# Mixture-of-experts rows placed by scatter in DRAM without index lists, and the decay mixer's constants moved among its first steps

## What is computed

```python
# L0_ffn: attention, then one of four experts for each row
x = x + _attn(x, ...)
h = _layernorm(x, ln2_w, ln2_b)
expert_idx = jnp.argmax(h @ router_w, axis=-1)
for e in range(4):
    gate_raw, value = jnp.split(h @ expert_wv[e], 2, axis=-1)      # 256 -> 2 x 1024
    y = gate_raw * sigmoid(gate_raw) * value @ expert_proj[e]       # 1024 -> 256
    out = out + jnp.where((expert_idx == e)[..., None], y, 0.0)
# L1_attn: the decay mixer: layer norm, W_in, a causal convolution of 4 taps, silu, a second norm,
# then a decaying mix whose rates come from A = clip(log(1 + exp(A_param)), 0.1, 10)
```

## Time and profile before

| What | us |
|---|---|
| three runs, lowest, median, highest | 3326.74, 3329.53, 3329.79 |
| the profiled execution's own time | 3336.9 |
| its span, from first to last instruction | 3335.1 |
| PE busy | 2797.5 (84%) |
| DVE busy | 2184.5 (65%) |
| ACT busy | 1569.1 (47%) |
| POOL busy | 1043.2 (31%) |

### The profile page before, as it was taken

How to read it: one execution, slowest core, us unless ns; L and a number is a source line. 1 busy time by engine, 2 the same in 40 slices (tenths; PEclk the granted TensorE clock), 3 DMA queues, 4 the chain that set the end, 5 groups by cost and what they waited for, 6 DMA issues and landing times.

```text
span 3335.1 us, 40739 instructions
## 1 busy us (share of the span) xinstructions
PE 2797.5 (84%) x13719; PEld 1686.9 (51%) x13782; DVE 2184.5 (65%) x3943; ACT 1569.1 (47%) x2311; POOL 1043.2 (31%) x705
## 2 busy tenths in 40 slices
PE   7778887787764699999966999948988887999999
PEld 3444454454452355555543666624444444666666
DVE  0698898899893676777532222226777775777776
ACT  2677667766761245555541111137777782111111
POOL 0887787788871111112102111012111100010000
PEclk9898998999866899999988999978999998999999
DMA  3354444454552744555323000010000002000000
GB/s 108 80 112 107 105 104 103 96 113 103 111 110 61 105 70 83 86 89 95 63 104 81 26 23 23 17 49 13 7 7 7 7 1 58 7 7 13 7 7 13
DMA packets 120347, 198.60 MB, mean 60 GB/s; under 512 B 15728, under 2 KB 78064, under 8 KB 118992
## 3 DMA queue, kind: packets, MB, share of 16 engines
q1 hardware_dynamic: 97504, 124.24, 16.5%
q0 software_dynamic: 22640, 71.75, 10.9%
HBM read 107.12 MB, written 25.91 MB: 40 GB/s over the span
## 4 chain that ended last, share of the span: by engine, by line
PE 51%; ACT 5%; DVE 5%; issue 4%; DMA 2%; POOL 0%; SPq 0%; ACTq 0%; DVEq 0%; POOLq 0%
PE PS L1517 7%; PE PS L2222 7%; PE PS L2240 6%; PE PS L1539 4%; PE PS L1810 3%; PE PS L1182 2%; PE PS L1859 2%; ACT Z L1963 2%; PE PS L1817 2%; PE PS L1161 2%; PE PS L1164 2%; PE PS L1109 1%; PE PS L1139 1%; PE PS L1877 1%; PE PS L1208 1%
## 5 line engine op out<-in xcount | busy, mean ns | idle before, releaser
L702 POOL TENSOR_TENSOR Z<-Z 128x1024 f32<-128x1024 f32 x256 | 652.7, 2661 | 109.5 <-PE PS L472 109.3
L652 DVE TENSOR_TENSOR_SCAN Z<-PS,Z 128x1024 f32<-128x1024 f32 x256 | 583.3, 2279 | 7.7 <-ACT PS L584 7.7
L472 PE MATMUL PS<-Z 128*128 128x128 f32 x2048 | 313.9, 301 | 139.8 <-DVE Z L665 131.9
L472 PEld LDWEIGHTS PS<-Z 128*128 128x128 f32 x2048 | 259.1, 156 | 288.4 <-DVE Z L652 145.2
L584 ACT ACTIVATE PS<-Z 128x511 f32<-128x511 f32 x512 | 332.2, 683 | 91.9 <-DVE Z L652 91.0
L1275 ACT ACTIVATE Z<-PS 128x512 f32<-128x512 f32 x320 | 189.1, 597 | 262.5 <-PE PS L1164 259.0
L2222 PE MATMUL PS<-Z 128*128 128x512 f32 x576 | 273.8, 600 | 17.5 <-DVE Z L2355 17.5
L440 PE MATMUL PS<-Z 128*128 128x512 f32 x512 | 254.6, 614 | 36.3 <-ACT Z L519 35.6
L2273 ACT ACTIVATE Z<-PS 128x512 f32<-128x512 f32 x144 | 86.0, 597 | 416.8 <-PE PS L2222 416.8
L1370 DVE TENSOR_REDUCE Z<-PS 128x1 f32<-128x512 f32 (+2 forms) x384 | 182.7, 508 | 114.6 <-PE PS L1140 109.9
L1963 ACT ACTIVATE Z<-Z 128x2048 f32<-128x2048 f32 x128 | 252.7, 2000 | 10.3 <-PE PS L1859 8.5
(11 more groups left out here) (278 smaller groups left out, 5021.6 us busy)
## 6 DMA issues: line engine op xcount, KB each, us to landing
Z<-Z POOLq DMA_DIRECT2D x120, 512.0 KB, 4.6
Z<-rows_b SPq DMA_DIRECT2D x128, 256.0 KB, 3.1
Z<-scr SPq DMA_DIRECT2D x256, 128.0 KB, 5.7
scr<-Z SPq DMA_DIRECT2D x32, 384.0 KB
Z<-in_L_ffn_expert_wv SPq DMA_DIRECT2D x4, 2048.0 KB, 14.6
rows_y<-Z SPq DMA_DIRECT2D x35, 128.0 KB, 1.7
Z<-in_L_attn_x SPq DMA_DIRECT2D x8, 512.0 KB, 8.9
rows_n<-Z SPq DMA_DIRECT2D x8, 512.0 KB, 2.9
```

Source lines behind the costliest of these rows:

```text
L472: ins = e.transpose(o[:, c * 128:(c + 1) * 128], self.h(k, c // 2)[:, c % 2, i * 128:(i + 1) * 128], ident)
L652: e.tensor_tensor_scan(h, a, h, 0.0, ALU.mult, ALU.add).then_inc(s["scan"], 1)
L702: e.tensor_tensor(self.h(k, f), self.du[b % 2][:, 2 * f:2 * f + 2, :], b3(self.Bs[k % 2], 1, [128, 2, 512]), ALU.mult).then_inc(s["hin"], 1)
```

## The change

The array `lists` and all that serves it go away: the cleared buffer, SP's write of it, the scatter of row numbers, the 35 gathers of row numbers. `rows_n` grows from 4096 rows to four regions of 4224 rows, one for each expert, and POOL scatters the normalized rows themselves (1 KB each) to their places; SP's eight stores to `rows_n` go. So that places which no row takes hold numbers, POOL first copies part of the expert weights over the whole array, in four transfers from DRAM to DRAM of 4.3 MB each, right after step `low` of group 4 in stage B. `nt` and `h2` change tiles, and the waits with them. SP loads `we` once two heads are turned. In stage D the constants' work becomes steps among the first block's steps, whose plan is one unit longer.

```diff
-        self.lists = m.nc.dram_tensor("lists", [NE * self.REG, 1], I32, kind="Internal").ap()
-        self.rows_n = m.nc.dram_tensor("rows_n", [4096, 256], F32, kind="Internal").ap()
+        self.rows_n = m.nc.dram_tensor("rows_n", [NE * self.REG, 256], F32, kind="Internal").ap()
...
-        e.wait_ge(s["zero"], 1)
-        e.dma_start(self.lists.rearrange("(p n) o -> p (n o)", p=128), self.zero).then_inc(s["d_l"], 16)
...
             elif p == 3:
                 e.wait_ge(s["nb"], b + 1)
                 if b < NB - 1:
-                    e.wait_ge(self.b.s["pj"], 2 * (b + 1))
+                    e.wait_ge(self.b.s["hc"], min(b + 4, NB) + 1)
+                if 0 < b < NB - 1:
+                    e.wait_ge(s["d_rows"], 64 * b)
...
+    def pool(self, e):
+        size = self.REG * 256
+        some = self.m.d["L0_ffn_expert_wv"].rearrange("x k m -> (x k m)")[0:size].rearrange("(p n) -> p n", p=128)
+        for x in range(self.NE):
+            e.dma_start(self.rows_n[x * self.REG:(x + 1) * self.REG].rearrange("(p n) c -> p (n c)", p=128),
+                        some).then_inc(self.s["d_fill"], 16)
...
             if p == 10:
                 e.wait_ge(s["posi"], b + 1)
-                if b == 0:
-                    e.wait_ge(s["ready"], 1)
-                    e.wait_ge(s["d_l"], 16)
+                e.wait_ge(s["d_fill"], 16 * self.NE)
             c = 4 * b + p - 10
-            e.indirect_dma_start(self.lists, bass.IndirectOffsetOnAxis(ap=self.posi[:, c:c + 1], axis=0),
-                                 self.ids[:, c:c + 1], None).then_inc(m.d_lists, 16)
+            e.indirect_dma_start(self.rows_n, bass.IndirectOffsetOnAxis(ap=self.posi[:, c:c + 1], axis=0),
+                                 self.nt[b][p - 10], None).then_inc(s["d_rows"], 16)
...
         def flipped(b):
             if b >= 4:
-                e.wait_ge(*self.made["route", b - 4, 6])
+                e.wait_ge(*self.made["route", b - 4, 4, 1])
+                e.wait_ge(self.route.s["d_rows"], 64 * (b - 3))
...
+            if g == 4:
+                self.route.pool(e)
...
-        e.wait_ge(self.route.s["posi"], NB)
+        e.wait_ge(s["ht"], 2)
         for x in range(self.NE):
             e.dma_start(self.we[:, 2048 * x:2048 * (x + 1)].rearrange("p (k m) -> p k m", k=8), ...
...
-        e.wait_ge(m.d_lists, 16 * 4 * NB)
-        e.wait_ge(self.route.s["d_rows"], 16 * NB)
+        e.wait_ge(self.route.s["d_rows"], 64 * NB)
         def rows(c):
-            e.wait_ge(*self.d_li.done(c))
             if c >= 4:
                 e.wait_ge(s["ht"], c - 3)
             e.indirect_dma_start(self.gr[c % 4], None, self.rows_n,
-                                 bass.IndirectOffsetOnAxis(ap=self.li[c % 4].bitcast(I32), axis=0)).then_inc(
+                                 bass.IndirectOffsetOnAxis(ap=self.start[:, c:c + 1], axis=0)).then_inc(*self.d_gr.over(c))
...
+    START = (
+        (("stats",), ("consts",)), (("rstd",), ("minus",), ("spread",)), (("norm",), ("decay",)), (("flip", 0), ("flip", 1)),
+        (("flipped", 0), ("flipped", 1), ("lift", 2)), (("lifted", 2), ("lift", 3)),
+        (("lifted", 3), ("taps", 2), ("lift", 0)), (("lifted", 0), ("taps", 3), ("lift", 1)), (("bound",),),
+        (("lifted", 1), ("conv", 0)), (("conved", 0), ("conv", 1))) + PLAN[10:]
```

More of the change, by code:

```diff
@@ L734, in __init__ @@
         self.upf = ar.take([128])
-        self.tab = ar.take([32 + 35 + 8 + 1 + 32])
-        self.ids = ar.take([32]).bitcast(I32)
+        self.tab = ar.take([32 + 35 + 8 + 1])
         self.oh = ar.take([32, 4])
@@ L988, in __init__ @@
         for b in range(NB - 1):
-            self.route.nt[b] = self.yf.rearrange("p a (b c) -> p (a b) c", c=256)
-            self.route.h2[b] = self.hp[:, :, 2:514]
+            self.route.nt[b] = [self.hp[:, i // 2, 2 + 256 * (i % 2):258 + 256 * (i % 2)] for i in range(4)]
+            self.route.h2[b] = self.yf
         self.end_use = {}
@@ L1081, in load @@
                                     self.d_stack[which][w % 3], 16)
-        self.walk(low=low, load=load, route=self.route.sp_steps(e))
+        self.walk(low=low, load=load)
     def pe(self, e):
@@ L1444, in __init__ @@
         self.nt, self.h2 = ar.take([4, 256]), ar.take([2, 512])
-        route.nt[NB - 1], route.h2[NB - 1] = self.nt, self.h2
-        self.li = [ar.take([1]) for _ in range(4)]
+        route.nt[NB - 1], route.h2[NB - 1] = [self.nt[:, i, :] for i in range(4)], self.h2
         self.gr = [ar.take([256]) for _ in range(4)]
@@ L1462, in __init__ @@
         for c in range(NS + 1):
-            for what, i in (("ups", c), ("fetch", c + 4), ("rows", c + 3), ("head", c + 2), ("downs", c - 1),
+            for what, i in (("ups", c), ("rows", c + 4), ("head", c + 2), ("downs", c - 1),
                             ("flips", c)):
@@ L1474, in sp, with load @@
         m, d, s = self.m, self.m.d, self.s
-        for x in range(self.NE):
+        def load(x):
             e.dma_start(self.wv[:, 4096 * x:4096 * (x + 1)].rearrange("p (k m) -> p k m", k=2),
                         d["L0_ffn_expert_wv"][x].rearrange("(k p) m -> p k m", p=128)).then_inc(self.d_cv, 16)
-        route = self.route.sp_steps(e)
-        for p in range(Route.PIECES):
-            route(NB - 1, p)
-        e.wait_ge(self.route.s["posi"], NB)
+        for x in range(self.NE):
+            load(x)
+        e.wait_ge(s["ht"], 2)
         for x in range(self.NE):
@@ L1674, in rows @@
             e.indirect_dma_start(self.gr[c % 4], None, self.rows_n,
-                                 bass.IndirectOffsetOnAxis(ap=self.li[c % 4].bitcast(I32), axis=0)).then_inc(
-                                     *self.d_gr.over(c))
+                                 bass.IndirectOffsetOnAxis(ap=self.start[:, c:c + 1], axis=0)).then_inc(*self.d_gr.over(c))
         for c in range(4):
-            fetch(c)
-        for c in range(3):
             rows(c)
-        self.walk(fetch=fetch, rows=rows)
+        self.walk(rows=rows)
 class StageD:
@@ L1767, in order @@
                     out += [("fetch", x), ("add", x)]
-                if at in range(len(self.PLAN)):
-                    out += [(s[0], x) + s[1:] for s in self.PLAN[at]]
+                plan = self.PLAN if x else self.START
+                if at in range(len(plan)):
+                    out += [(s[0], x) + s[1:] for s in plan[at]]
         return out
@@ L1788, in pe @@
         m, s, ring, ident = self.m, self.s, self.ring, self.m.ident
-        e.wait_ge(s["d_w"], 64)
-        e.wait_ge(s["consts"], 1)
         def bank(*step):
@@ L1813, in conv @@
         def conv(b, c):
+            e.wait_ge(s["consts"], 1)
             e.wait_ge(*ring.done(self.use("lift", b, c)))
@@ L1885, in act, with decay @@
         e.preload_act_table_set(LN_EXP)
-        e.wait_ge(s["d_a"], 64)
-        e.activation(self.An, self.An, ACT.Exp).then_inc(*own.tick())
-        e.wait_ge(*own.now())
-        e.activation(self.An, self.An, ACT.Ln, bias=m.one).then_inc(s["an"], 1)
         e.wait_ge(s["pads"], 1)
+        def decay(b):
+            e.wait_ge(s["d_a"], 64)
+            e.activation(self.An, self.An, ACT.Exp).then_inc(*own.tick())
+            e.wait_ge(*own.now())
+            e.activation(self.An, self.An, ACT.Ln, bias=m.one).then_inc(s["an"], 1)
         def evac(out, *step, func=ACT.Copy, **kw):
@@ L1969, in wout @@
             e.activation(self.wt[w % 2], self.wb[w % 2], ACT.Copy).then_inc(s["wt"], 1)
-        e.wait_ge(s["an"], 2)
-        self.walk(rstd=rstd, norm=norm, flipped=flipped, lifted=lifted, conved=conved, silu=silu, rstd2=rstd2, xf=xf,
+        self.walk(decay=decay, rstd=rstd, norm=norm, flipped=flipped, lifted=lifted, conved=conved, silu=silu, rstd2=rstd2, xf=xf,
                   soft=soft, grow=grow, wout=wout)
@@ L2083, in acc @@
             e.tensor_tensor(m.X[:, w, :], m.X[:, w, :], self.ob[:, 0:256], ALU.add).then_inc(s["acc"], 1)
-        self.walk(add=add, stats=stats, minus=minus, taps=taps, stats2=stats2, xn=xn, pj=pj, clip=clip, scalars=scalars,
+        self.walk(consts=consts, spread=spread, bound=bound, add=add, stats=stats, minus=minus, taps=taps, stats2=stats2, xn=xn, pj=pj, clip=clip, scalars=scalars,
                   scale=scale, gate=gate, acc=acc)
```

73 lines of the change are left out of this document (30 added, 43 removed).

## The result

The changed kernel is slower: 3357.23 us in the median of four runs (3349.8 to 3362.52), against 3328.19 us of the kernel before beside it (3326.74 to 3329.79). The ratio is 1.0086, with a 95% interval from 1.0062 to 1.0109. The prediction of 3313.6 us and "faster" was wrong. The profiled execution took 3353.41 us, with a span of 3351.5.

What follows compares the result with a forecast made beforehand. PE was taken as the bound (84% of the span), so only its waits could shrink. Terms -3.6 + 6.4 - 13.1 - 5.6 = -15.9 us took 3336.9 to 3321.0, less 7.4 for the median: 3313.6 us, range 3303 to 3355.

Steps and rivals of the forecast that it cites:

- the fill in B: Stage B, POOL's four copies beside the stack loads: 0.2 us lost per transfer, 32 transfers, +6.4 us (0 to +61).
- rival 1: Stage B: the fill's long rows shut out the stack load's small packets for 41 to 82 us; slower, chance 0.27.
- The start of B: SP issues `sel` earlier without the cleared list's write, so DVE's conversion comes sooner: -3.6 us (0 to -3.7).
- The scatters in B: Stage B: POOL scatters 1 KB rows instead of 4-byte numbers, SP drops eight stores, waits move: cost nothing.
- The start of C: Row scatters land earlier, first gather issues when DVE's long add ends, first head sooner: -13.1 us (-10.8 to -16.8).
- Rival 2: Start of C: row scatters land as late as before, only the hop over numbers is saved; 7.2 us less, chance 0.26.
- The start of D: Adds of gathered rows overlap their landing and constants move later, so the norm comes sooner: -5.6 us (-2.6 to -7.6).

Runs made afterwards that it cites:

- fill_alone: The kernel before plus the same four fill transfers at the same place, into an array that nobody reads: 3373.06 us, ratio 1.012.

## Why the prediction was wrong

**The step that failed is the fill in B**: "So a transfer loses 0.2 us mostly, 1.9 at worst", times 32, +6.4 us, with ends 0 and +61. Measured, PE's wait grew by 49.62 - 3.96 = 45.7 us, and `fill_alone` gives 40.3 for the stage. The value of 0.2 came from a row in which SP's load runs beside 4 KB rows of POOL, and I carried it over to rows eight times as long, although rival 1 had named that very difference. The reason given for the low value, that the path had room, was beside the point: the wait is set by the turns (372 packets for 371), not by the bandwidth that is free. Rival 1 was the case that came, and its form was right (the load does not move while the copy runs, "over 35, with traffic near the copy's rate"). It had a chance of 0.27 only; its time of 3348 or more holds 3357.2, and the range stopped at 3355, inside it. Its packets were not single rows, as it took them, but 45 KB in the mean.

**The start of B**: -3.6 predicted; the conversion of `sel` came 10.07 us after the stage's start in place of 13.49, -3.4.

**The scatters in B, "cost nothing"**: B without the fill's wait is some 7 us shorter than this and the start of B give, so the term is off on the good side if the 7 us are of these edits. It is not shown that they are: the stores and the wait `pj` are excluded, the small scatters cost as much in one run, and `fill_alone` has them without the loss.

**The start of C**: -13.1 predicted, -13.0 measured, and step by step. The row scatters were landed 25.6 us after `wv` (24.3 taken), the first gather was issued at the end of DVE's long add, and the head came 3.2 us behind that add (3.0 taken). `we` behind the second head delayed nothing. Rival 2 fell: the scatters of rows land in 6 us, not 16, beside the same long add; whether because they are of 1 KB or because `we` no longer loads beside them is not shown, and the prediction did not name `we` for it.

**The start of D**: -5.6 predicted; the stage was 4.3 us shorter in this trace and the first lift 4.3 us sooner (24.4 in place of 28.7). The norm came 6.4 us sooner (17.4 after the start, before 23.7), not 9.4, because the gathers landed as late as 13.4 us after the start for the last add, where I took 10.2 (2195.5). So the gain was smaller; what `decay` gave back by the first lift was 6.4 - 4.3 = 2.1, where I took 2.8 and another 1.0 for the clock.

With the fill at its true price the sum is -3.4 + 45.7 - 3.8 - 13.8 - 4.3 = +20.4 on the span, where -3.8 is what else B gained (38.5 + 3.4 - 45.7). That rest is no term of its own: in `fill_alone`, where nothing but the fill was added, the wait grew by 48.4 and the stage by 40.3, so what PE waits there and what the stage grows by differ by 8 us without any other edit. The span grew by 16.4; the other -4.0 is stage A, whose code is the same (the load of the router's weights, 2.4 us into B, came between 1021 and 1045 us in these traces). The medians differ by 29.0; the 8.6 us beyond the sum no trace shows.

## What to carry to other kernels

Price a transfer beside another queue by the size of its packets, not by the bandwidth that is free: here a large contiguous copy all but shut a queue of 1 KB packets out until it was over, and rows contiguous in source and target were joined whatever the shape in the code. Put such a copy where nothing is waiting for the DMA engines, or cut it, and then see whether its engine stands still after many issues (here after 18). A gather on GpSimd should not be issued beside one long two-input VectorE instruction; cut the instruction and spread it.

## What the runs showed of the hardware

- Two queues with work shared the DMA engines packet for packet: 371 to 372 packets in 45 us with packets of 39 KB against 0.9 KB (means, small ones included), 1765 to 1755 in 25 us with 4.0 against 0.9 KB.
- The contiguous copy of 17.3 MB travelled in 384 packets of 45 KB in the mean; in rows of 4 KB cut out of longer ones in 4224; in rows of 1 KB in 4224 again.
- That copy from DRAM to DRAM, beside the load that it held up, ran at 340 to 347 GB/s for both together (1124 to 1156). PE's granted clock fell to 0.50 (1.2 GHz) while it stood still, and was 0.51 in the 20 us after the wait.
- POOL issued 18 copies of up to 1024 rows of 1 KB in 12.9 us and then stood for 49.2 us before the next.
- The same kernel gave stage D at 582 and at 594 us in two executions, and stage A, never changed, ended anywhere in a range of 24 us. B was steadier: 680.4 to 683.6 in five runs whose B is the same.
